# Cross-attention by autocorrelation with a LoRA-mixed feed-forward layer: the two residual adds on GpSimd become accumulating DMAs

## The chip, the cores and the metric

One core of one Trainium2 chip runs the whole kernel. The metric is the device time in microseconds (us). The engines are TensorE (PE in the profile; its weight loads are PEld), VectorE (DVE), ScalarE (ACT), GpSimd (POOL) and SyncE (SP), which here issues every DMA.

## The reference

Cut to what matters, with x and ctx of shape (8, 512, 2048):

```python
def reference(x, ctx, W, bias, A, Bf, coeffs, scales):
    q, v = heads(layernorm(x)), heads(ctx)          # keys and values are both ctx; 8 heads
    corr = irfft(fft(q) * conj(fft(v)))             # over the 512 positions, per column
    w, idx = top_k(corr, int(2 * log(512)))         # 12 lags for each column
    w = softmax(w)
    x = x + sum_i w[i] * v[min(idx[i] + position, 511)]
    h = layernorm(x)
    x = x + h @ W.T + bias                          # the FFN
    x = x + sum_e coeffs[e] * scales[e] * (h @ A[e].T) @ Bf[e].T
    return x
```

## The kernel before

**The work in windows.** A chunk is one batch element and 256 of the 2048 columns, so a batch element has eight chunks and there are 64. The program is one software pipeline of 78 windows and a closing step (`for w in range(windows + 1)` on every engine). Window w transforms chunk w (`values`, `upper`, `queries`), correlates it (`correlate`), picks its lags on VectorE (`choose`), turns the lag weights (`turn_weights`), and finishes chunk w - 1 (`upper_lags`, `lower_lags`, `output`, `part_output`, `store_parts`). From window 14 on, each window also holds an eighth of one batch element's feed-forward product: 96 fp16 matmuls of 128x512 into `f_ps` (`product`; L840, L842 and L844, since W and the normalised rows are each split into a high and a low half). The weights W plus the mixed LoRA update are made in windows 1 to 9.

**The rows.** A batch element has four tiles of 128 rows. Tile i of element b has its turn in window 9 + 8b + i (`row_tile`), so windows 9 to 12, 17 to 20, 25 to 28, 33 to 36 and so on up to 65 to 68 are "row windows", two buffers `rows` taking turns. In such a window SP loads the rows of x, POOL adds the attention (`add_row`), SP stores the sum to DRAM (`store_x1`), DVE takes its mean and variance (`row_statistics`, `row_gain`), ACT normalises it, and its two fp16 halves go to DRAM to come back transposed. The attention's rows come from the DRAM scratch `parts` into the one buffer `attn`, by `load_attn` on SP: the next tile's load is issued right behind the x1 store, ahead of the weights' transposes.

**The groups.** The product's output is finished in groups of 512 columns x 512 rows, one in every second window (`finished_group`). For a group, SP loads the column scales, the bias (broadcast over the partitions) and the stored sum `x1p`; at the end of the window POOL adds the bias to `x1p` (`add_bias`). In the next window DVE scales the product into `y` (`scale_group`), POOL adds it (`add_group`), and SP stores the group and loads the next one into the same buffers.

**Order.** Each engine works through a list written out by hand. Three lists matter here.

POOL in a window: `add_products` (writes `a_prod`), `add_group` if a group is due (in row windows: the second and fourth of a batch element), `add_upper`, `add_lower`, `add_row`, `fold_queries`, `fold_values`, `add_bias` (the first and third row window).

SP, from the row on: `store_x1`, which waits for `row_added`; `load_attn` of the next tile; `turn_weights`, two DMA transposes of `a_w_row` into `a_w_lag` (L515); one pair of weight loads; `load_v`; `store_parts`.

DVE, from `choose` on: `weights_low` (L1338), `row_statistics` (L1372), `part_output` (L1365, L1366; TensorE's `queries` waits for it), `row_gain`, then in the next window `scale_group`, `multiply_queries` (POOL's `add_products` waits for it), `multiply_upper`, `multiply_lower`.

TensorE opens window w + 1 with `upper_lags(w)`, the first matmul of L763, which waits for both transposes of window w.

Of the kernel before, what the change touches and what calls it, by code (L numbers as in the profile page):

```python
# [34 lines left out]
T = 128  # L35
BATCH, L, D = 8, 512, 2048
TB = L // T
WC = 512
# [193 lines left out]
def flow(nc, shared, x, W, A, Bf, coeffs, scales, parts, x1s, hrow, bias, whi, wlo, wscale, out):  # L232
# [12 lines left out]
    with ExitStack() as ctx:  # L245
# [20 lines left out]
        b_in_sb = w_sb[:, 2:4, :].rearrange("p a d -> p (a d)").rearrange("p (e i r) -> p e i r", e=EXPERTS, i=OT)  # L266
        attn = sb("f_attn", [T, D])
        row_hi = sb("f_rowhi", [T, D], F16)
# [5 lines left out]
        y = sb("f_y", [T, TB, WC])  # L274
        x1p = sb("f_x1p", [T, TB, WC])
        scale_sb = sb("f_scale", [T, WC])
        bias_sb = sb("f_bias", [T, WC])
        f_bn = sb("f_bn", [T, 4, 6])
# [131 lines left out]
        x1_out = sem("f_x1_out")  # L410
        attn_in = sem("f_attn_in")
        row_added = sem("f_row_added")
# [12 lines left out]
        y_added = sem("f_y_added")  # L425
        x1p_in = sem("f_x1p_in")
        scale_in = sem("f_scale_in")
        bias_in = sem("f_bias_in")
        bias_added = sem("f_bias_added")
# [41 lines left out]
        def _(sp):  # L471
# [22 lines left out]

            def load_attn(r, early):

                if r >= TILES:
                    return
                at_least(sp, row_added, r)
                if r == 0 and early:  # L500
                    sp.wait_ge(delta_mm, TB * OT)
                cols = slice(0, D) if r % TB else slice(0, D - CH) if early else slice(D - CH, D)
                sp.wait_ge(parts_out, 16 * (CHUNKS * (r // TB + 1) - (r % TB == 0 and early)))
                sp.dma_start(attn[:, cols], part_rows[r * T:(r + 1) * T, cols]).then_inc(attn_in, 16)

            def store_parts(n):
# [11 lines left out]
            def store_x1(w, r):  # L518
                sp.wait_ge(row_added, r + 1)
                sp.dma_start(x1s[r * T:(r + 1) * T, :], rows[w % 2][:, :]).then_inc(x1_out, 16)  # L520
# [37 lines left out]
            def load_group(g):  # L558

                if g >= 4 * BATCH:  # L560
                    return
                b, cols = g // 4, slice(g % 4 * WC, (g % 4 + 1) * WC)
                at_least(sp, y_done, TB * g)
                sp.dma_start(scale_sb[:, :], wscale[cols].partition_broadcast(T)).then_inc(scale_in, 16)
                at_least(sp, bias_added, g)
                sp.dma_start(bias_sb[:, :], bias[cols].partition_broadcast(T)).then_inc(bias_in, 16)
                at_least(sp, out_out, 16 * g)
                sp.wait_ge(x1_out, 16 * TB * (b + 1))
                sp.dma_start(x1p[:, :, :], x1s[b * L:(b + 1) * L, cols].rearrange("(i p) d -> p i d", p=T)
                             ).then_inc(x1p_in, 16)  # L570

            def store_group(g):
                b, cols = g // 4, slice(g % 4 * WC, (g % 4 + 1) * WC)
                if g == 4 * BATCH - 1:
# [70 lines left out]
            for w in range(windows + 1):  # L645
# [5 lines left out]
                load_x(w + 3)  # L651
                if r is not None and r % TB == 0:
                    load_attn(r, False)
                if made:
# [16 lines left out]
                if r is not None:  # L671
                    store_x1(w, r)
                    if r % TB < TB - 1:
                        load_attn(r + 1, True)
                if made:
# [32 lines left out]
                if 1 <= w <= N:  # L708
                    store_parts(w - 1)
                if w >= CHUNKS and w % CHUNKS == 0 and w // CHUNKS <= BATCH:  # L710
                    load_attn(TB * (w // CHUNKS - 1), True)
            sp.wait_ge(out_out, 16 * (4 * BATCH - 1 + TB))
# [397 lines left out]
        def _(pool):  # L1110
# [70 lines left out]
            def add_row(w, r):  # L1181

                pool.wait_ge(rows_in[w % 2], 16 * rows_job(w))
                pool.wait_ge(attn_in, 16 * (r + r // TB + 2))
                add(rows[w % 2][:, :], attn[:, :], ALU.add).then_inc(row_added, 1)

            def add_bias(g):

                pool.wait_ge(x1p_in, 16 * (g + 1))
                pool.wait_ge(bias_in, 16 * (g + 1))  # L1190
                add(x1p[:, :, :], bias_sb[:, :].unsqueeze(1).broadcast_to([T, TB, WC]), ALU.add
                    ).then_inc(bias_added, 1)

            def add_group(g):

                pool.wait_ge(bias_added, g + 1)
                for t in range(TB):
                    pool.wait_ge(y_done, TB * g + t + 1)
                    add(x1p[:, t, :], y[:, t, :], ALU.add).then_inc(y_added, 1)
# [40 lines left out]
        def _(dve):  # L1240
# [127 lines left out]
            def row_statistics(w, r):  # L1368

                dve.wait_ge(row_added, r + 1)  # L1370
                for j in range(4):
# [24 lines left out]
            def scale_group(g):  # L1396

                dve.wait_ge(scale_in, 16 * (g + 1))
                for t in range(TB):
                    dve.wait_ge(product_mm, TB * g + t + 1)  # L1400
                    at_least(dve, y_added, TB * (g - 1) + t + 1)
                    product(y[:, t, :], f_ps[:, t, :], scale_sb[:, :]).then_inc(y_done, 1)

# [142 lines left out]
```

## Time and profile before

| | us |
|---|---|
| median of 3 runs | 2646.56 (2642.76 to 2648.35) |
| span of the profiled execution | 2644.4 |
| TensorE matmuls busy | 2497.7 (94%) |
| GpSimd busy | 2155.5 (82%) |
| VectorE busy | 1901.7 (72%) |
| ScalarE busy | 1055.7 (40%) |
| SP's DMA queue, share of 16 engines' span | 76.6% |

The profiled execution's own span is 2.2 us under the median; no separate device time is given for it. An engine's busy time leaves out waiting, branches and the issuing of DMAs. Matmuls are pipelined and their ends are modelled, so the times between starts say more than durations do. A time to landing of a DMA runs from its issue to its completion.

### The profile page before, as it was taken

Reading aid. Unit: us, or ns where it says so; the run is one execution under the profiler, and the core shown is the slowest. Engines: PE = TensorE matmul, PEld = TensorE weight load, DVE = VectorE, ACT = ScalarE, POOL = GpSimd, SP = SyncE. Lnnn points to the kernel's source line nnn. Section 1 sums busy time; section 2 is a strip of 40 time slices with the busy share of each in tenths; the row PEclk is TensorE's granted clock in tenths of the full one; section 3 lists DMA queues with packets and bytes.
Section 4 is the critical chain, followed back from the end, with each engine's and each line's share of the span. In section 5 each row is a group of like instructions: output and inputs, shape, how many; then the busy total and the mean of one; then the engine's idle time right before and its main releaser. Section 6 shows DMA issues by size and latency. Waiting matters only on the chain.

```text
span 2644.4 us, 36606 instructions
## 1 busy us (share of the span) xinstructions
PE 2497.7 (94%) x12288; PEld 1559.9 (59%) x12288; DVE 1901.7 (72%) x4966; ACT 1055.7 (40%) x1906; POOL 2155.5 (82%) x1558
## 2 busy tenths in 40 slices
PE   4999866799999999999999999999999999999998
PEld 3655555566666656666666666666666666654444
DVE  5989989778787788777877788778876688645000
ACT  4788855533443343533443334533333233201000
POOL 5799999778998799988998899888998899654222
PEclk8999978899999999999999999999999999999999
DMA  9399998966788687966887687957786687758853
GB/s 325 99 261 269 269 244 198 231 192 209 254 266 228 219 252 238 277 203 210 258 270 210 217 275 248 271 181 236 253 250 172 219 265 243 199 203 301 268 180 114
DMA packets 550028, 613.19 MB, mean 232 GB/s; under 512 B 322640, under 2 KB 448720, under 8 KB 532176
## 3 DMA queue, kind: packets, MB, share of 16 engines
q1 hardware_dynamic: 549840, 610.86, 76.6%
q8 instruction: 97, 1.59, 0.2%
q14 instruction: 91, 0.75, 0.1%
HBM read 383.22 MB, written 151.00 MB: 202 GB/s over the span
## 4 chain that ended last, share of the span: by engine, by line
PE 53%; POOL 22%; DVE 8%; DMA 7%; SPq 5%; issue 4%; ACT 1%; POOLq 0%; DVEq 0%; ACTq 0%
PE f_ps L840 11%; PE f_ps L844 11%; PE f_ps L842 11%; PE a_ps L718 7%; PE a_ps L805 5%; PE a_ps L763 4%; POOL a_zu L1115 4%; POOL f_x1p L1115 4%; POOL a_rows L1115 3%; DMA a_w_lag<-a_w_row 2%; PE a_ps L821 2%; PE a_ps L820 2%; POOL a_zv L1115 2%; POOL a_zf L1115 2%; PE a_ps L768 1%
## 5 line engine op out<-in xcount | busy, mean ns | idle before, releaser
L840 PE MATMUL f_ps<-f_whi,f_hhi 128*128 128x512 f16 x2048 | 777.3, 380 | 5.6 <-issue 2.4
L844 PE MATMUL f_ps<-f_whi,f_hlo 128*128 128x512 f16 x2048 | 777.4, 380 | 0.0
L842 PE MATMUL f_ps<-f_wlo,f_hhi 128*128 128x512 f16 x2048 | 777.4, 380 | 0.0
L924 ACT ACTIVATE a_side<-a_ps 128x256 f32<-128x256 f32 (+1 forms) x320 | 128.0, 416 | 873.5 <-PE a_ps L805 698.4
L844 PEld LDWEIGHTS f_ps<-f_whi,f_hlo 128*128 128x128 f16 x2048 | 200.6, 98 | 242.3 <-issue 1.1
L842 PEld LDWEIGHTS f_ps<-f_wlo,f_hhi 128*128 128x128 f16 x2048 | 200.7, 98 | 230.8 <-issue 1.1
L840 PEld LDWEIGHTS f_ps<-f_whi,f_hhi 128*128 128x128 f16 x2048 | 200.7, 98 | 220.6 <-issue 6.7
L1115 POOL TENSOR_TENSOR a_prod<-a_prod,a_tf 128x512 f32<-128x512 f32 x128 | 160.2, 1273 | 138.7 <-DVE a_tf L1242 138.7
L1115 POOL TENSOR_TENSOR a_zv<-a_zv,a_tw 128x512 f32<-128x512 f32 x128 | 183.3, 1450 | 100.5 <-DVE a_tf L1242 100.5
L805 PE MATMUL a_ps<-inv,a_prod 128*128 128x256 f32 x1024 | 239.5, 388 | 25.6 <-POOL a_prod L1115 25.6
L1115 POOL TENSOR_TENSOR f_x1p<-f_x1p,f_y 128x512 f32<-128x512 f32 x128 | 172.7, 1381 | 101.0 <-DVE f_y L1242 101.0
L763 PE MATMUL a_ps<-a_w_lag,lags 128*128 128x256 f16 x1536 | 232.3, 274 | 23.0 <-DMA a_w_lag<-a_w_row 18.0
L805 PEld LDWEIGHTS a_ps<-inv,a_prod 128*128 128x128 f32 x1024 | 198.6, 195 | 65.2 <-POOL a_prod L1115 32.0
L1242 DVE TENSOR_TENSOR f_y<-f_ps,f_scale 128x512 f32<-128x512 f32 x128 | 81.0, 686 | 186.2 <-PE f_ps L844 169.5
L1115 POOL TENSOR_TENSOR f_x1p<-f_x1p,f_bias 128x2048 f32<-128x2048 f32 x32 | 147.5, 4608 | 69.8 <-DMA f_x1p<-x_scratch 69.8
L763 PEld LDWEIGHTS a_ps<-a_w_lag,lags 128*128 128x128 f16 x1536 | 149.7, 98 | 69.0 <-DMA a_w_lag<-a_w_row 23.4
L1115 POOL TENSOR_TENSOR a_zu<-a_zu,a_tu 128x512 f32<-128x512 f32 x128 | 172.3, 1367 | 5.1 <-DVE a_tu L1242 5.1
L1115 POOL TENSOR_TENSOR a_rows<-a_rows,f_attn 128x2048 f32<-128x2048 f32 x32 | 144.2, 4507 | 36.1 <-DMA f_attn<-parts_scratch 36.1
L1115 POOL TENSOR_TENSOR a_zf<-a_zf,a_tf 128x512 f32<-128x512 f32 x128 | 159.2, 1262 | 0.0
L1115 POOL TENSOR_TENSOR a_zu<-a_zu,a_zv 128x512 f32<-128x512 f32 x128 | 158.9, 1257 | 0.0
L718 PE MATMUL a_ps<-a_tv,fold 128*128 128x256 f32 x512 | 129.6, 398 | 26.8 <-ACT a_vk L924 26.8
L1026 ACT ACTIVATE a_rows<-a_rows,f_shift,f_gain 128x2048 f32<-128x2048 f32 x32 | 67.0, 2095 | 218.1 <-DVE f_shift L1384 154.9
(137 smaller groups left out, 5236.6 us busy)
## 6 DMA issues: line engine op xcount, KB each, us to landing
f_whi<-whi_scratch SPq DMA_DIRECT2D x128, 512.0 KB, 5.1
f_wlo<-wlo_scratch SPq DMA_DIRECT2D x128, 512.0 KB, 6.5
a_rows<-in_x_dram SPq DMA_DIRECT2D x62, 1024.0 KB, 8.7
vs<-in_ctx_dram SPq DMA_DIRECT2D x64, 512.0 KB, 6.2
xs<-in_x_dram SPq DMA_DIRECT2D x64, 512.0 KB, 8.0
parts_scratch<-a_so SPq DMA_DIRECT2D x64, 512.0 KB, 7.5
x_scratch<-a_rows SPq DMA_DIRECT2D x32, 1024.0 KB, 5.1
f_x1p<-x_scratch SPq DMA_DIRECT2D x32, 1024.0 KB, 6.8
```

The source lines that it names most:

```text
L718: return nc.tensor.matmul(ps[:, pair, j, :], fold[:, k, :], source, start=True, stop=True)
L763: mm = nc.tensor.matmul(out, lag_mat[:, constant, 2 * cls + k, :], w_lag[:, part, main::TB, :], start=(constant + part == 0), stop=(consta ...
L805: mm = nc.tensor.matmul(corr[:, g, cls * 2 * T:(cls + 1) * 2 * T], prod[:, 2 * k + cls, g * T:(g + 1) * T], inv[:, cls, k, :], start=(k == ...
L820: nc.tensor.matmul(ps[:, 2 + j, i, :], outm[:, k0, :], z[:, s0, :], start=True, stop=False)
L821: mm = nc.tensor.matmul(ps[:, 2 + j, i, :], outm[:, k1, :], z[:, s1, :], start=False, stop=True)
L840: nc.tensor.matmul(f_ps[:, t, :], h_hi[q][:, kq, rows_t], w_hi[u % WR][:, :, kq, :], start=(k == 0), stop=False)
L842: nc.tensor.matmul(f_ps[:, t, :], h_hi[q][:, kq, rows_t], w_lo[u % WR][:, :, kq, :], start=False, stop=False)
L844: mm = nc.tensor.matmul(f_ps[:, t, :], h_lo[q][:, kq, rows_t], w_hi[u % WR][:, :, kq, :], start=False, stop=(k == DB - 1))
L924: return nc.scalar.activation(out, source, ACT.Copy, **how)
L1026: nc.scalar.activation(rows[w % 2][:, :], rows[w % 2][:, :], ACT.Identity, bias=f_shift[:, 0:1], scale=f_gain[:, 0:1]).then_inc(h_done, 1)
L1115: return nc.gpsimd.tensor_tensor(whole, whole, part, op)
L1242: return nc.vector.tensor_tensor(out, a, b, ALU.mult)
```

## The change

`attn` and its loads disappear. `add_row` is now a DMA, issued by GpSimd, that reads 128 rows of `parts` from DRAM and adds them to `rows` in SBUF. `add_bias` is a DMA, issued by GpSimd, that reads the bias broadcast over 128 partitions and four row tiles (the source is 512 rows of 2 KB, 1 MB written) and adds it to `x1p`. `row_added` and `bias_added` are now raised by these transfers' completion. `add_row` also waits for the DMA before it and for the element's parts to be stored in full. `x1p` and the scales have two buffers each, taken in turn by group, so a group's loads wait for the group before the last.

```diff
-        attn = sb("f_attn", [T, D])
-        x1p = sb("f_x1p", [T, TB, WC])
-        scale_sb = sb("f_scale", [T, WC])
-        bias_sb = sb("f_bias", [T, WC])
+        x1ps = [sb(f"f_x1p{i}", [T, TB, WC]) for i in range(2)]
+        scales_sb = [sb(f"f_scale{i}", [T, WC]) for i in range(2)]
...
-            def load_attn(r, early):
...
             def store_x1(w, r):
-                sp.wait_ge(row_added, r + 1)
+                sp.wait_ge(row_added, 16 * (r + 1))
                 sp.dma_start(x1s[r * T:(r + 1) * T, :], rows[w % 2][:, :]).then_inc(x1_out, 16)
...
             def load_group(g):
...
-                at_least(sp, y_done, TB * g)
-                sp.dma_start(scale_sb[:, :], wscale[cols].partition_broadcast(T)).then_inc(scale_in, 16)
-                at_least(sp, bias_added, g)
-                sp.dma_start(bias_sb[:, :], bias[cols].partition_broadcast(T)).then_inc(bias_in, 16)
-                at_least(sp, out_out, 16 * g)
+                x1p = x1ps[g % 2]
+                at_least(sp, y_done, TB * (g - 1))
+                sp.dma_start(scales_sb[g % 2][:, :], wscale[cols].partition_broadcast(T)).then_inc(scale_in[g % 2], 16)
+                at_least(sp, out_out, 16 * (g - 1))
                 sp.wait_ge(x1_out, 16 * TB * (b + 1))
                 sp.dma_start(x1p[:, :, :], x1s[b * L:(b + 1) * L, cols].rearrange("(i p) d -> p i d", p=T)
-                             ).then_inc(x1p_in, 16)
+                             ).then_inc(x1p_in[g % 2], 16)
...
-                if r is not None and r % TB == 0:
-                    load_attn(r, False)
...
                     store_x1(w, r)
-                    if r % TB < TB - 1:
-                        load_attn(r + 1, True)
...
-                if w >= CHUNKS and w % CHUNKS == 0 and w // CHUNKS <= BATCH:
-                    load_attn(TB * (w // CHUNKS - 1), True)
...
             def add_row(w, r):
 
                 pool.wait_ge(rows_in[w % 2], 16 * rows_job(w))
-                pool.wait_ge(attn_in, 16 * (r + r // TB + 2))
-                add(rows[w % 2][:, :], attn[:, :], ALU.add).then_inc(row_added, 1)
+                at_least(pool, row_added, 16 * r)
+                pool.wait_ge(parts_out, 16 * CHUNKS * (r // TB + 1))
+                pool.dma_start(rows[w % 2][:, :], part_rows[r * T:(r + 1) * T, :], accum_op=ALU.add
+                               ).then_inc(row_added, 16)
 
             def add_bias(g):
 
-                pool.wait_ge(x1p_in, 16 * (g + 1))
-                pool.wait_ge(bias_in, 16 * (g + 1))
-                add(x1p[:, :, :], bias_sb[:, :].unsqueeze(1).broadcast_to([T, TB, WC]), ALU.add
-                    ).then_inc(bias_added, 1)
+                cols = slice(g % 4 * WC, (g % 4 + 1) * WC)
+                pool.wait_ge(x1p_in[g % 2], 16 * (g // 2 + 1))
+                pool.dma_start(x1ps[g % 2][:, :, :], bias[cols].partition_broadcast(T).unsqueeze(1).broadcast_to([T, TB, WC]),
+                               accum_op=ALU.add).then_inc(bias_added, 16)
 
             def add_group(g):
 
-                pool.wait_ge(bias_added, g + 1)
+                x1p = x1ps[g % 2]
+                pool.wait_ge(bias_added, 16 * (g + 1))
...
             def row_statistics(w, r):
 
-                dve.wait_ge(row_added, r + 1)
+                dve.wait_ge(row_added, 16 * (r + 1))
```

`scale_group` and `store_group` take the buffer and semaphore of `g % 2` in the same way.

## Rows read from the trace of the kernel before

**Rows 1.** Busy time of each engine in four windows: start:end, length, then each engine.

```profile
687.58:725.57 37.99, 37.99 (x185) 23.86 (x186) 29.29 (x77) 13.04 (x27) 32.49 (x24) 0.96 0.72 235
...
1240.48:1279.62 39.14, 36.46 (x185) 23.05 (x183) 33.89 (x82) 15.91 (x29) 38.83 (x26) 1.00 0.88 284
1279.62:1316.42 36.80, 36.47 (x184) 23.08 (x185) 29.68 (x78) 13.82 (x28) 33.26 (x25) 1.00 0.79 238
...
1389.03:1425.33 36.30, 36.30 (x185) 23.15 (x184) 24.90 (x71) 14.81 (x32) 29.99 (x26) 1.00 0.97 273
```

**Rows 2.** What TensorE waited for from 520 to 2310 us: total, times, longest.

```profile
PE a_ps L763 <- DMA a_w_lag<-a_w_row: 18.0, 10, 4.0
```

**Rows 3.** TensorE's timeline: `upper_lags` opening windows 19, 35, 37; `queries` before one.

```profile
687.58 0.50 PE L763 MATMUL a_ps<-a_w_lag,lags 128*128 128x256 f16 x3 [3.01 <-DMA a_w_lag<-a_w_row]
...
1275.05 1.89 PE L718 MATMUL a_ps<-xs,fold 128*128 128x256 f32 x8
...
1279.62 0.50 PE L763 MATMUL a_ps<-a_w_lag,lags 128*128 128x256 f16 x3 [2.69 <-DMA a_w_lag<-a_w_row]
...
1352.73 0.49 PE L763 MATMUL a_ps<-a_w_lag,lags 128*128 128x256 f16 x3
```

**Rows 4.** SP's timeline, from the x1 store on, in windows 34 and 36.

```profile
1269.76 0.33 SPq L520 DMA_DIRECT2D x_scratch<-a_rows  x1
1270.19 0.38 SPq L504 DMA_DIRECT2D f_attn<-parts_scratch  x1
1270.66 6.88 SPq L515 DMA_TRANSPOSE a_w_lag<-a_w_row  x2
...
1346.23 4.34 SPq L515 DMA_TRANSPOSE a_w_lag<-a_w_row  x2
```

**Rows 5.** POOL's timeline: the four row adds of windows 33 to 36, one bias.

```profile
1224.11 4.51 POOL L1115 TENSOR_TENSOR a_rows<-a_rows,f_attn 128x2048 f32<-128x2048 f32 x1
...
1240.12 4.57 POOL L1115 TENSOR_TENSOR f_x1p<-f_x1p,f_bias 128x2048 f32<-128x2048 f32 x1
1244.66 2.49 POOL L1115 TENSOR_TENSOR a_prod<-a_prod,a_tf 128x512 f32<-128x512 f32 x2
...
1265.23 4.50 POOL L1115 TENSOR_TENSOR a_rows<-a_rows,f_attn 128x2048 f32<-128x2048 f32 x1
...
1300.10 4.51 POOL L1115 TENSOR_TENSOR a_rows<-a_rows,f_attn 128x2048 f32<-128x2048 f32 x1
...
1341.27 4.52 POOL L1115 TENSOR_TENSOR a_rows<-a_rows,f_attn 128x2048 f32<-128x2048 f32 x1
```

**Rows 6.** DVE's timeline: row statistics of windows 33 to 35, and work behind them.

```profile
1231.94 2.46 DVE L1372 BATCH_NORM_STATS2 f_bn<-a_rows 128x6 f32<-128x512 f32 x4
...
1242.76 0.68 DVE L1242 TENSOR_TENSOR a_tf<-a_ps,a_vk 128x512 f32<-128x512 f32 x1
...
1269.77 2.47 DVE L1372 BATCH_NORM_STATS2 f_bn<-a_rows 128x6 f32<-128x512 f32 x4 [1.45 <-POOL a_rows L1115]
...
1273.26 0.68 DVE L1366 TENSOR_TENSOR a_so<-a_ps,a_side 128x512 f32<-128x512 f32 x1
...
1307.39 2.46 DVE L1372 BATCH_NORM_STATS2 f_bn<-a_rows 128x6 f32<-128x512 f32 x4
```

**Rows 7.** DMA issues: count, KB each, median us to landing.

```profile
x_scratch<-a_rows SPq DMA_DIRECT2D x32, 1024.0 KB, 5.1
f_x1p<-x_scratch SPq DMA_DIRECT2D x32, 1024.0 KB, 6.8
...
f_attn<-parts_scratch SPq DMA_DIRECT2D x24, 1024.0 KB, 7.7
```

**Rows 8.** POOL's timeline in window 11, before the product starts.

```profile
421.57 4.50 POOL L1115 TENSOR_TENSOR a_rows<-a_rows,f_attn 128x2048 f32<-128x2048 f32 x1
...
437.87 2.51 POOL L1115 TENSOR_TENSOR a_prod<-a_prod,a_tf 128x512 f32<-128x512 f32 x2 [0.25 <-DVE a_tf L1242]
```

**Rows 9.** TensorE's timeline, in the last batch element's product.

```profile
2470.54 0.38 PE L840 MATMUL f_ps<-f_whi,f_hhi 128*128 128x512 f16 x1 [2.35 <-issue]
```

More of the change, by code:

```diff
@@ L410, in flow @@
         x1_out = sem("f_x1_out")
-        attn_in = sem("f_attn_in")
         row_added = sem("f_row_added")
@@ L425, in flow @@
         y_added = sem("f_y_added")
-        x1p_in = sem("f_x1p_in")
-        scale_in = sem("f_scale_in")
-        bias_in = sem("f_bias_in")
+        x1p_in = [sem(f"f_x1p_in{i}") for i in range(2)]
+        scale_in = [sem(f"f_scale_in{i}") for i in range(2)]
         bias_added = sem("f_bias_added")
@@ L493, in load_rows @@
                 sp.dma_start(rows[w % 2][:, :], x_rows[source * T:(source + 1) * T, :]).then_inc(rows_in[w % 2], 16)
-            def load_attn(r, early):
[L497 to L504, printed above, removed]
             def store_parts(n):
@@ L1183, in add_row @@
                 pool.wait_ge(rows_in[w % 2], 16 * rows_job(w))
-                pool.wait_ge(attn_in, 16 * (r + r // TB + 2))
-                add(rows[w % 2][:, :], attn[:, :], ALU.add).then_inc(row_added, 1)
+                at_least(pool, row_added, 16 * r)
+                pool.wait_ge(parts_out, 16 * CHUNKS * (r // TB + 1))
+                pool.dma_start(rows[w % 2][:, :], part_rows[r * T:(r + 1) * T, :], accum_op=ALU.add
+                               ).then_inc(row_added, 16)
             def add_bias(g):
-                pool.wait_ge(x1p_in, 16 * (g + 1))
-                pool.wait_ge(bias_in, 16 * (g + 1))
-                add(x1p[:, :, :], bias_sb[:, :].unsqueeze(1).broadcast_to([T, TB, WC]), ALU.add
-                    ).then_inc(bias_added, 1)
+                cols = slice(g % 4 * WC, (g % 4 + 1) * WC)
+                pool.wait_ge(x1p_in[g % 2], 16 * (g // 2 + 1))
+                pool.dma_start(x1ps[g % 2][:, :, :], bias[cols].partition_broadcast(T).unsqueeze(1).broadcast_to([T, TB, WC]),
+                               accum_op=ALU.add).then_inc(bias_added, 16)
             def add_group(g):
-                pool.wait_ge(bias_added, g + 1)
+                x1p = x1ps[g % 2]
+                pool.wait_ge(bias_added, 16 * (g + 1))
                 for t in range(TB):
@@ L1396, in scale_group @@
             def scale_group(g):
-                dve.wait_ge(scale_in, 16 * (g + 1))
+                dve.wait_ge(scale_in[g % 2], 16 * (g // 2 + 1))
                 for t in range(TB):
@@ L1401, in scale_group @@
                     at_least(dve, y_added, TB * (g - 1) + t + 1)
-                    product(y[:, t, :], f_ps[:, t, :], scale_sb[:, :]).then_inc(y_done, 1)
+                    product(y[:, t, :], f_ps[:, t, :], scales_sb[g % 2][:, :]).then_inc(y_done, 1)
             def first_statistics(k, source):
```

## The prediction

> **What bounds the kernel now.** I read the busy times of each engine window by window first. With the product running, a window without a row lasts 36.30 us and TensorE is busy for all of it; POOL is busy for 30 [rows 1]. So TensorE sets the pace, and POOL's 82% is no bound by itself. Then the waits of TensorE from 520 to 2310 us, six of the eight batch elements: one kind only, `upper_lags` waiting for the transposed lag weights, 18.0 us in ten waits, 4.0 the longest [rows 2]. All ten follow row windows. That is the place where the row's work touches the clock that counts.
>
> The timelines of window 34 say how. POOL adds the row until 1269.73 [rows 5]. SP stands on `row_added` until then, then issues the x1 store, the load of the next `attn` and only then the transposes, which take SP 6.88 us [rows 4]; the lags start at 1279.62, after 2.69 us of waiting [rows 3]. So 9.9 us lie between the end of the add and the lags. In window 36 no `attn` load stands ahead: the add ends at 1345.79, the transposes take SP 4.34 us [rows 4], and the lags start at 1352.73 without a wait [rows 3, 5]. There 6.9 us are enough.
>
> A stall has a second price. After the wait of 3.01 us at 687.58 the window lasts 37.99 us at a mean granted clock of 0.96 [rows 1, 3]: for part of it TensorE runs at 1.2 instead of 2.4 GHz. That is 1.7 us over 36.30. After 2.69 us the clock stays at 1.00. I charge 1.7 us to each stall of 3 us or more. In the six elements before, that is the one shown and the one of 4.0: 3.4 us. The row windows thus cost 18.0 + 3.4 = 21.4 us over pure TensorE pace. This is nearly all that the change could win there.
>
> **What the change does, part by part.** POOL loses 4.5 us per row and 4.6 us per bias [rows 5]. Inside a row window the row add was the last thing before SP's transposes, so what counts is not POOL's time but the time from the DMA's issue to `row_added`. Call it L; it was 4.5.
>
> No row shows an accumulating DMA, nor one issued by POOL. Below: it can't well beat the fastest plain 1 MB transfer, the x1 store's 5.1 us. Above: two plain passes, since it reads its target as well, 2 x 7.7 = 15.4. The plain read of this very source takes 7.7 at the median [rows 7]. I take L = 10: the plain read, plus about 2.3 for the second operand and for descriptors written by software, between the ends but nearer to 7.7 because a second read of SBUF need not repeat the latency.
>
> The Trainium skill (DMA: Bandwidth & Descriptors, section Bandwidth) gives 6.15 us of DMA time for a plain 1 MB load issued by GpSimd, with a first byte after about 1 us; by that, for a transfer that doesn't accumulate, L would be 7.2, and the sum below would end at about no change. No run here shows it yet.
>
> Now the four row windows of an element, using 33 to 36. POOL reaches the row add at 1224.11, 1265.23, 1300.10 and 1341.27 [rows 5]; the next window opens 6.9 us after `row_added`, or on TensorE's pace, whichever is later.
>
> Window 33: ready at 1224.11 + L + 6.9; TensorE opened at 1240.48 [rows 1]. Stall L - 9.5, for L = 10: 0.5.
>
> Behind it on DVE: the statistics started at 1231.94 [rows 6], so they slip by L - 7.8 = 2.2, and behind them `part_output`, `row_gain`, `scale_group`, `multiply_queries`. The last ended at 1243.44; POOL's `add_products` ran only at 1244.66, behind the bias [rows 5, 6]. With the bias off POOL it gains 1.2 and loses 2.2: POOL is 1.0 later in window 34.
>
> Window 34: ready at 1265.23 + 1.0 + 10 + 6.9 = 1283.1. TensorE's pace is 1279.62 - 2.69 + 0.5 = 1277.4. Stall 5.7.
>
> Window 35 has no group. POOL's add came 20.5 us after the window's opening [rows 3, 5], with DVE's last product of the lags as the releaser, so it stays there: 20.5 + 10 + 6.9 - 36.3 = 1.1.
>
> Window 36: the statistics before it slip by L - 7.3 (1307.39 against 1300.10), less the same 1.2: 1.5. POOL's add stood 25.35 us behind the undelayed opening (1279.62 + 36.30 = 1315.92). Stall 25.35 + 1.5 + 16.9 - 36.3 - 1.1 = 6.35.
>
> Sum per element 13.7, plus 2 x 1.7 for the clock, 17.1; six elements 102.4, less the 21.4 of before: +81. Behind SP's wait for `row_added` stand the transposes, a pair of weight loads, `load_v`, `store_parts` and the next window's `load_x`; the weights loaded there are for the second half of the window after, 18 us away, and hide. Part of the stall may be seen one step earlier: `part_output` ended 4.2 us after the add in window 34 and `queries` starts 1.1 us later (1273.94, 1275.05) [rows 3, 6], so it waits too. It is the same delay, not a second one.
>
> Element 0's rows (windows 9 to 12) meet no product. There from the row add to the next `add_products` it is 16.3 us, all POOL work [rows 8], ended within 0.25 us of DVE. The new path runs over DVE: from the statistics at 1231.94 to the end of the queries' products at 1243.44 it is 11.5, of which the four multiplications of `scale_group`, absent here, are about 2.3 [rows 6]. So L + 9.2 = 19.2, +2.9. Windows 11 and 12 pay it, +6; 9 and 10 also hold a `tile_low` on POOL whose removal from the path about balances it.
>
> Element 7's rows run beside the product alone. No `attn` load is waited for any more, and the group loads no longer hold SP, so the stall of 2.35 at 2470.54 [rows 9] may go: -2.
>
> The bias: POOL can issue it 4.5 earlier than 1240.12, at 1235.6; `add_group` would begin at 1247.1 + 1.0 [rows 5]. Up to 12.5 us of landing are hidden; its like (2 KB runs of 1 MB) takes 6.8 plain [rows 7], 13.6 in two passes. I take 0, with POOL's slack as cover. Second buffers and the dropped waits of SP: 0, since SP's transposes don't wait for them in row windows. The extra traffic rests in L.
>
> Total +81 + 6 - 2 = +85 on a span of 2644.4; on the median, 2646.6 + 85 = 2731 to 2732. I say 2731.
>
> The same sum for other L: 5.1 gives -27; 7 gives -7; 7.3 about 0; 8 gives +23 (stalls 0, 2.2, 0, 3.45; one at the low clock); 12 gives +147 (2.5, 7.7, 3.1, 8.35); 15.4 gives +246.
>
> **Rivals.** *The transfer is as quick as a plain one* (L 5.1 to 7.2). For it: stores of 1 MB take 5.1, and the DMA no longer shares SP's order. Against: the plain read takes 7.7, and this one does more. All row stalls go except 1 to 2 us. Result 2620 to 2642, faster. It decides at L = 7.3.
>
> *A much slower transfer* (L 13 to 15.4): adding in the DMA runs at half the rate, or POOL's writing of descriptors is stretched. For it: the DMA share is already 0.72 to 0.88 in the three row windows shown [rows 1]. Result about 2830 to 2893. The Trainium skill (SBUF — State Buffer, section SBUF: two separate sides) says a VectorE operation in a two-port mode keeps GpSimd from writing the descriptors of its DMAs; that would act here, and no row before can show it.
>
> *The bias is late.* If it lands after 15.4 instead of under 12.5, `add_group` and with it the rows of windows 34 and 36 come 3 us later: 12 x 3 = +36 on top, 2767. For it: 512 runs of 2 KB in the stretch where SP issues weights, values and queries together. Against: 12.5 leaves 5.7 us over the plain landing, more than I charge the row's transfer for its adding.
>
> *Nothing to be measured*: L between 7.2 and 7.5.
>
> **Numbers.** Chances: my forecast (L 8 to 13, bias hidden) 0.53, its own range 2664 to 2830; bias late 0.14; much slower 0.14; quick 0.14; nothing 0.05. Faster by over 0.2% (5 us, about what can be told from no change) 0.14, within 0.05, slower 0.81. The range for 8 in 10 takes in the upper part of the quick case and half of the much slower one: 2635 to 2855.
>
> **What would show it.** L itself: the DMA's issue to landing. `upper_lags` waiting about 6 us after the second and fourth row window of an element and near 1 after the others; windows of 42 to 44 us there, clock 0.96 or less; POOL's busy share down to about 68% (2155.5 less 32 x 9.1); DVE waiting for the DMA before L1372, SP before the x1 store. No stall above 2 us and L near 7 would prove me wrong, as would a wait of TensorE for weights or `h` because the queues are full.

## The result, and the profile after

The changed kernel takes 2740.64 us (median of 4 runs, 2734.85 to 2742.42) against 2644.66 (2641.53 to 2648.35): 1.0357 of the time before, with a 95% interval of 1.0342 to 1.0372. That is 96 us slower; the prediction said 2731. The profiled executions stand 94.3 us apart. One run of `e7_best` took 5345.51 us, twice its three others, and is left out of its time below.

```profile
span 2738.7 us, 36462 instructions
...
PE 2534.0 (93%) x12288; PEld 1577.1 (58%) x12288; DVE 1894.6 (69%) x4966; ACT 1055.7 (39%) x1906; POOL 1924.3 (70%) x1558
```

GpSimd lost 231 us of busy work and the kernel became slower. First the windows 33 to 37, which answer to [rows 1]: start:end, length, each engine's busy time with instructions, granted clock, DMA share, GB/s.

```profile
1233.71:1270.01 36.30, 36.30 (x185) 23.15 (x184) 31.08 (x92) 10.45 (x22) 27.63 (x24) 1.00 0.62 175
1270.01:1314.52 44.51, 38.20 (x185) 24.04 (x184) 31.23 (x80) 13.64 (x28) 32.44 (x26) 0.96 0.90 263
1314.52:1350.82 36.30, 36.30 (x185) 23.18 (x184) 30.52 (x79) 15.33 (x28) 28.72 (x23) 1.00 0.82 232
1350.82:1395.62 44.80, 39.66 (x186) 24.92 (x185) 31.37 (x81) 13.95 (x28) 32.11 (x26) 0.93 0.92 271
1395.62:1432.16 36.54, 36.54 (x185) 23.33 (x184) 27.10 (x63) 24.16 (x41) 28.19 (x22) 0.99 0.92 266
```

The first and third row windows stand at TensorE's pace. The second and fourth, which also hold a group add, last 44.5 and 44.8 us. In all six batch elements it is these twelve windows, 42.5 to 45.7 us each; together they last 533.0 us, against 455.2 before. They account for 77.8 of the 94.3 us; the tail behind the last window with attention work gives 8.6, the rest of the windows about 8.

What TensorE waited for from 520 to 2391 us (total, times, longest), beside [rows 2]:

```profile
PE a_ps L697 <- DVE a_so L1348: 42.8, 12, 4.9
PE a_ps L799 <- POOL a_zu L1094: 26.2, 20, 2.6
PE a_ps L742 <- DMA a_w_lag<-a_w_row: 0.4, 1, 0.4
```

The transposes, on which TensorE had waited 18.0 us, are almost gone from the list. The delay now shows one step earlier, twelve times, as `queries` waiting for `part_output` (a_so), and there is a wait of another kind: `output` for POOL's `a_zu`. TensorE's timeline in window 34 has both:

```profile
1297.53 0.67 PE L799 MATMUL a_ps<-a_zu,outm 128*128 128x256 f32 x2 [1.41 <-POOL a_zu L1094]
...
1311.29 3.39 PE L697 MATMUL a_ps<-xs,fold 128*128 128x256 f32 x8 [4.89 <-DVE a_so L1348]
1314.52 0.49 PE L742 MATMUL a_ps<-a_w_lag,lags 128*128 128x256 f16 x3
```

The window is 8.21 us too long: 6.30 of waiting, and 1.90 because its matmuls are busy for 38.20 instead of 36.30 us. Most of these 1.90 are in one row: the eight matmuls of `queries` take 3.39 us after the wait, where they took 1.89 before [rows 3]. The granted clock over them is 0.55: TensorE fell from 2.4 to 1.2 GHz behind a wait of 4.89 us. (Windows with a wait show 36.5 to 36.7 us of busy matmuls at a clock of 1.00 too, so 0.2 to 0.4 of the 1.90 is not the clock.)

Why `part_output` is late, on POOL, beside [rows 5]:

```profile
1265.78 1.28 POOL L1172 DMA_DIRECT2D f_x1p<-in_L_ffn_bias_dram  x1
1273.06 2.50 POOL L1094 TENSOR_TENSOR a_prod<-a_prod,a_tf 128x512 f32<-128x512 f32 x2 [6.01 <-DVE a_tf L1224]
1279.22 7.00 POOL L1094 TENSOR_TENSOR f_x1p<-f_x1p,f_y 128x512 f32<-128x512 f32 x4 [3.66 <-DMA f_x1p<-in_L_ffn_bias_dram]
...
1297.33 0.60 POOL L1165 DMA_DIRECT2D a_rows<-parts_scratch  x1
```

The bias was issued at 1265.78 and landed at about 1279.2, 13.4 us later. The group add waited 3.66 us for it, everything behind it moved back, and the row's DMA went out at 1297.33, 27.3 us into the window. The 7.00 us of the group add are no loss beside the kernel before; the section on the early bias shows why. SP, beside [rows 4], in windows 33 and 34:

```profile
1261.21 0.32 SPq L505 DMA_DIRECT2D x_scratch<-a_rows  x1
1261.62 4.40 SPq L500 DMA_TRANSPOSE a_w_lag<-a_w_row  x2
...
1306.96 0.33 SPq L505 DMA_DIRECT2D x_scratch<-a_rows  x1
1307.39 4.35 SPq L500 DMA_TRANSPOSE a_w_lag<-a_w_row  x2
```

The x1 store follows `row_added` at once, so issue to `row_added` is 27.50 - 19.94 = 7.56 us in window 33 (issue at 1253.65) and 36.95 - 27.32 = 9.63 in window 34. And DVE, beside [rows 6]:

```profile
1261.47 2.46 DVE L1354 BATCH_NORM_STATS2 f_bn<-a_rows 128x6 f32<-128x512 f32 x4
...
1280.29 2.35 DVE L1376 TENSOR_TENSOR f_rowlo<-a_rows,f_rowhi 128x2048 f16<-128x2048 f32 x1
```

In window 33 the statistics start without a wait: a row transfer of 7.56 us is wholly hidden there. The DMA issues, beside [rows 7] (count, KB each, median us to landing), and the queues (packets, MB, share of 16 engines):

```profile
q1 hardware_dynamic: 539472, 568.91, 68.9%
q0 software_dynamic: 21504, 67.11, 13.4%
...
a_rows<-parts_scratch POOLq DMA_DIRECT2D x32, 1024.0 KB, 8.3
x_scratch<-a_rows SPq DMA_DIRECT2D x32, 1024.0 KB, 4.3
f_x1p<-x_scratch SPq DMA_DIRECT2D x32, 1024.0 KB, 9.1
f_x1p<-in_L_ffn_bias_dram POOLq DMA_DIRECT2D x32, 1024.0 KB, 14.0
```

### The profile page after: what moved, and what is told of

Same layout as the page of the kernel before. It is cut to its first block and busy times, and to the rows that moved or that the text cites. A ratio compares the mean times of both kernels' runs of the same rounds, so it can differ in the third digit from the quotient of the medians.

```text
span 2738.7 us, 36462 instructions
## 1 busy us (share of the span) xinstructions
PE 2534.0 (93%) x12288; PEld 1577.1 (58%) x12288; DVE 1894.6 (69%) x4966; ACT 1055.7 (39%) x1906; POOL 1924.3 (70%) x1558
## 3 DMA queue, kind: packets, MB, share of 16 engines
q0 software_dynamic: 21504, 67.11, 13.4%
## 5 line engine op out<-in xcount | busy, mean ns | idle before, releaser
L1094 POOL TENSOR_TENSOR f_x1p<-f_x1p,f_y 128x512 f32<-128x512 f32 x128 | 182.3, 1454 | 268.6 <-DMA f_x1p<-in_L_ffn_bias_dram 165.1
L697 PE MATMUL a_ps<-xs,fold 128*128 128x256 f32 x512 | 146.4, 437 | 65.2 <-DVE a_so L1348 65.1
L1354 DVE BATCH_NORM_STATS2 f_bn<-a_rows 128x6 f32<-128x512 f32 x128 | 79.1, 681 | 153.4 <-DMA a_rows<-parts_scratch 152.9
L697 PEld LDWEIGHTS a_ps<-xs,fold 128*128 128x128 f32 x512 | 109.3, 219 | 98.3 <-issue 66.4
L1094 POOL TENSOR_TENSOR a_zu<-a_zu,a_tu 128x512 f32<-128x512 f32 x128 | 159.8, 1270 | 4.6 <-DVE a_tu L1224 4.6
```

The costliest lines, as they stand in the source:

```text
L697: return nc.tensor.matmul(ps[:, pair, j, :], fold[:, k, :], source, start=True, stop=True)
L1094: return nc.gpsimd.tensor_tensor(whole, whole, part, op)
L1354: op = nc.vector.bn_stats(f_bn[:, j, :], rows[w % 2][:, j * WC:(j + 1) * WC])
```

## The experiments

The theory after this reading (A): two costs, the row's transfer between row and transposes, and the bias that lands too late for the group add; the bias is the larger. The rivals: (B) the row's transfer alone makes the loss, because it adds and is slow, and the bias only follows; (C) the order behind the row on SP and DVE makes it, and neither transfer would cost anything elsewhere. These letters are of this section; each recorded expectation has its own. The ratios are to the kernel before, run beside each experiment (medians of 2645.64 to 2648.12 us).

### One part alone

`e1_row_only`: the row by DMA, the bias by POOL as before (with two x1p buffers).

```diff
-                pool.dma_start(x1ps[g % 2][:, :, :], bias[cols]...broadcast_to([T, TB, WC]),
-                               accum_op=ALU.add).then_inc(bias_added, 16)
+                pool.wait_ge(bias_in, 16 * (g + 1))
+                add(x1ps[g % 2][:, :, :], bias_sb[:, :].unsqueeze(1).broadcast_to([T, TB, WC]), ALU.add
+                    ).then_inc(bias_added, 1)
```

> The row is added by the DMA as in the changed kernel, the bias is loaded by SP and added by GpSimd as before (x1p keeps its two buffers, the scales have one). Theory A, the row's latency and a late bias both cost: in the row windows with a group, GpSimd issues the row about 2.5 us earlier in the window than in the changed kernel (it no longer waits for the bias), twelve times, and the small waits of output() in the other group windows go: 2740 - 30 - 8 = about 2700 to 2706. Theory B, only the row's latency costs (as the prediction has it, bias at nothing): about 2740. Theory C, the bias is the main part: under 2670.

`e2_bias_only`: the kernel before, with only `add_bias` made a DMA (one x1p buffer).

```diff
-                pool.wait_ge(bias_in, 16 * (g + 1))
-                add(x1p[:, :, :], bias_sb[:, :].unsqueeze(1).broadcast_to([T, TB, WC]), ALU.add
-                    ).then_inc(bias_added, 1)
+                pool.dma_start(x1p[:, :, :], bias[cols]...broadcast_to([T, TB, WC]),
+                               accum_op=ALU.add).then_inc(bias_added, 16)
```

> The kernel before, with the bias alone added by a DMA that GpSimd issues (one x1p buffer, rows added by GpSimd from attn). Theory A: the bias lands some 13 us after its issue, add_group begins 2 to 4 us later in every group window, and in the row windows with a group the lag weights' transposes and so TensorE come later by that: +35 to +60 us, 2680 to 2705. Theory B: GpSimd loses 4.6 us per group and the bias is hidden: 2635 to 2645. Theory C: over 2710.

Measured: the row alone 2659.2 us, 1.0043 (1.0026 to 1.0059), so about +11; the bias alone 2740.14 us, 1.0355 (1.0334 to 1.0375), so +94 by the ratio, as much as the whole change. Both lie where the expectations put the bias as the main part (under 2670, over 2710), and outside the 2700 to 2706 and 2680 to 2705 that I favoured. Window 34 of the row alone, then its waits of TensorE from 540 us:

```profile
1245.99:1284.37 38.38, 36.70 (x185) 23.00 (x184) 30.30 (x78) 12.86 (x27) 32.73 (x27) 1.00 0.89 273
```

```profile
PE a_ps L701 <- DVE a_so L1352: 18.9, 12, 2.5
PE a_ps L746 <- DMA a_w_lag<-a_w_row: 8.5, 13, 2.1
```

No wait is above 2.5 us, and the granted clock is 0.99 or 1.00 in the twelve second and fourth row windows. It is 0.97 in window 21 and 0.96 in window 27, which together last 2.8 us more than 36.30 each. Window 27 opens after a wait of 2.13 us, with one of 1.46 shortly ahead of it; before, a single wait of 2.69 us left the clock at 1.00. So the length of one wait doesn't tell what the clock does. Window 34 of the bias alone, on POOL:

```profile
1266.45 1.32 POOL L1188 DMA_DIRECT2D f_x1p<-in_L_ffn_bias_dram  x1
...
1280.54 4.94 POOL L1112 TENSOR_TENSOR f_x1p<-f_x1p,f_y 128x512 f32<-128x512 f32 x4 [8.17 <-DMA f_x1p<-in_L_ffn_bias_dram]
...
1296.60 4.49 POOL L1112 TENSOR_TENSOR a_rows<-a_rows,f_attn 128x2048 f32<-128x2048 f32 x1
```

The row add is POOL's own, and starts at 29.8 us into the window instead of 24.75 [rows 5], because the group add waits 8.17 us for the bias. TensorE's waits from 520 to 2391 us:

```profile
PE a_ps L817 <- POOL a_zu L1112: 63.6, 15, 6.2
PE a_ps L760 <- DMA a_w_lag<-a_w_row: 13.1, 6, 3.7
```

So the late group add holds TensorE in two ways: through `add_upper` and `add_lower` behind it on POOL, which write the `a_zu` that `output` needs, and through the row. Here the first is the larger. B falls. The parts don't add up (11 + 94 against 96): with one x1p buffer the bias can go out only 0.38 us ahead of window 34; with two, 4.23 ahead. The second buffer thus gives the bias's DMA a start of some 4 us. That this closes the sum is argued, since no run has the bias alone with two buffers.

### The bias issued earlier

`e4_bias_early`: the changed kernel, with the bias's DMA ahead of `add_upper` in the same window, some 28 us earlier.

```diff
+                if at and at[1] % 2 == 1:
+                    add_bias(4 * at[0] + at[1] // 2)
                 if 1 <= w <= N:
                     add_upper(w - 1)
...
-                if at and at[1] % 2 == 1:
-                    add_bias(4 * at[0] + at[1] // 2)
```

> The changed kernel with the bias DMA issued on GpSimd ahead of add_upper in the same window instead of at the window's end, so that it has some 30 us to land. Theory A: the wait of add_group for the bias (165 us in all) goes, rows are issued some 2.5 us earlier in twelve windows: 2700 to 2710. Theory B: no change, 2740, or worse where GpSimd now waits for x1p in front of add_upper.

Measured: 2673.92 us, 1.01 (1.0082 to 1.0118). One moved issue gives back 67 of the 96 us, twice what was expected (2700 to 2710). The transfer is hardly quicker (12.1 us at the median against 14.0), but nobody waits for it; window 34 has the row-only kernel's 38.40 us, and the row's DMA goes out 23.65 us into the window and lands 8.08 later, against 27.32 and 9.63. TensorE's waits from 540 us:

```profile
PE a_ps L697 <- DVE a_so L1348: 19.2, 12, 3.1
PE a_ps L742 <- DMA a_w_lag<-a_w_row: 8.4, 13, 2.2
PE a_ps L742 <- DVE a_tf L1224: 0.3, 1, 0.3
```

The waits for `a_zu` are gone as well. The group add now takes 4.96 us instead of 7.00, but the add behind it takes longer by as much, as it does with the row alone:

```profile
1258.74 4.54 POOL L1094 TENSOR_TENSOR a_zu<-a_zu,a_tu 128x512 f32<-128x512 f32 x2
```

In the changed kernel this add took 2.49 us. DVE's `f_rowlo` (1280.29 above) falls on one of the two adds in either case and costs it 2.05 us. So the whole 3.67 us by which the row's DMA goes out later (27.32 against 23.65) is the group add's wait for the bias. The late bias costs that, 1.5 us in this row's transfer, and the low clock. The kernel is still 15 us above the row alone, 9 of them behind the last window with the attention's work: that tail lasts 347.6 us in the changed kernel, 348.6 here, 339.2 with the row alone and 339.0 before.

### What makes the two transfers long

`e3_row_plain`: the row's DMA without `accum_op`, otherwise the changed kernel. x's own part of the residual is left out.

```diff
-                pool.dma_start(rows[w % 2][:, :], part_rows[r * T:(r + 1) * T, :], accum_op=ALU.add
-                               ).then_inc(row_added, 16)
+                pool.dma_start(rows[w % 2][:, :], part_rows[r * T:(r + 1) * T, :]).then_inc(row_added, 16)
```

> The changed kernel, but the row's DMA overwrites the row of x instead of adding to it (the residual of x is left out). It tells what the adding costs within the transfer. Theory A: little, the plain load of the same bytes took 7.7 us to landing before and this one takes 8.3 to 9.6: L shorter by about 0.5 us, twelve windows, 2730 to 2736. Rival: the second operand makes up the 2.3 us that the prediction charged for it and more: L near 6, 2700 to 2715.

Measured: 2694.56 us, 1.0177 (1.0161 to 1.0193). Issue to `row_added` is 5.10 us in window 33 and 7.46 in window 34, against 7.56 and 9.63: adding costs the transfer 2.2 to 2.5 us, and about 46 us of the kernel when the bias is late as well. Both expected ranges (2730 to 2736, 2700 to 2715) were too high; the rival was nearer.

`e8_bias_plain`: the bias's DMA without `accum_op`; x and the attention are left out of those outputs. `e9_bias_rows`: its source is 512 different runs of x1 in DRAM instead of one 2 KB run read 512 times; the bias is left out and x1 counts twice.

```diff
-                pool.dma_start(x1ps[g % 2][:, :, :], bias[cols].partition_broadcast(T).unsqueeze(1).broadcast_to([T, TB, WC]),
-                               accum_op=ALU.add).then_inc(bias_added, 16)
+                # e8_bias_plain: the same call without accum_op
+                # e9_bias_rows: source x1s[g // 4 * L:(g // 4 + 1) * L, cols].rearrange("(i p) d -> p i d", p=T)
```

> The changed kernel, but the bias DMA overwrites x1p instead of adding to it (x and the attention are left out of the result). It tells what the adding costs in this transfer, which lands 13.4 us after its issue. If the adding is the main cost (as 2.5 us of 7.6 is in the row's transfer), it lands within 9 to 10 us and the run comes near the one with the early bias, 2675 to 2690. If the 512 runs of 2 KB and the traffic are, it still lands after 12 us or more: 2715 to 2740.

> The changed kernel, but the bias DMA adds 512 different runs of 2 KB (the stored x1, once more) instead of the same 2 KB read 512 times; the bias is left out of the result and x1 counts twice. It tells what makes this transfer land after 13 to 14 us. If reading one 2 KB place over and over is slow, it lands within 8 to 10 us and the run is at 2675 to 2700. If the short runs or the traffic around are the cause, it lands after 12 us or more as before: 2715 to 2745.

Measured: 2722.95 us, 1.0285 (1.027 to 1.0301), and 2731.96 us, 1.0334 (1.0313 to 1.0355), both in the second of the two ranges that were expected. The medians to landing of the bias's DMA, first plain, then from different rows:

```profile
f_x1p<-in_L_ffn_bias_dram POOLq DMA_DIRECT2D x32, 1024.0 KB, 12.5
```

```profile
f_x1p<-x_scratch POOLq DMA_DIRECT2D x32, 1024.0 KB, 13.8
```

Neither the adding (1.5 us) nor the repeated source (0.2) makes it late. What is left is what the three have in common: 1 MB in 512 runs of 2 KB on GpSimd's queue, in the stretch where SP issues weights, values and queries. The queue counts 144 packets for each row and 528 for each bias (4608 with the row alone, 16896 with the bias alone). The number of packets by itself doesn't set the time: in `e8_bias_plain` a bias has 272 (13312 packets less the rows' 4608, over 32) and lands only 1.5 us sooner. The stretch isn't the main cause either, since 28 us earlier in the window (`e4_bias_early`) it still takes 12.1. SP's load of `x1p`, also 1 MB in runs of 2 KB and plain, takes 9.1 in the changed kernel. What share the run length, the queue and the traffic have was not separated further.

### The order behind the row

`e5_late_both`: the changed kernel, with SP's transposes ahead of the x1 store, so that they don't stand behind `row_added`, and `part_output` ahead of the row statistics on DVE. `e6_before_late`: the same two moves in the kernel before (`load_attn` moves with the store). `e7_best`: both moves and the early bias.

```diff
-                if r is not None:
-                    store_x1(w, r)
                 if turned_by_dma(w):
                     turn_weights(w)
+                if r is not None:
+                    store_x1(w, r)
...
-                if r is not None:
-                    row_statistics(w, r)
                 if 1 <= w <= N:
                     part_output(w - 1)
+                if r is not None:
+                    row_statistics(w, r)
```

> The changed kernel with two moves that take row_added off TensorE's path: SP stores x1 behind the weights' transposes instead of ahead of them, and VectorE writes the output halves (part_output) ahead of the row's statistics. Theory A (a late row reaches TensorE only through these two waits; the late bias delays the row issue): the waits of queries() on a_so and the late lags go, what is left is the output() matmuls' wait for GpSimd, late through the bias: even row windows at 38 to 40 us instead of 44.5, about 2665 to 2685. Rival (the late bias holds TensorE by itself, through the product sums of GpSimd): above 2710.

> The kernel before with the same two moves (the next attn load moves with the x1 store). Theory A: the 18.0 us of waits for the transposes and the clock's 3.4 us go, so 2622 to 2630. Rival: the row windows are held by GpSimd's own load in any case, and it stays at 2640 to 2648.

> The changed kernel with both moves and the bias DMA issued ahead of add_upper. Theory A: no wait of TensorE between windows 14 and 62 is left, every window 36.3 us (1780 for these 49 instead of 1806 before): 2620 to 2635, if the last windows lose nothing; it then tells whether the accumulating DMAs gain anything over the kernel before with the same moves. Rival: DMA traffic in the row windows delays weights or transposes: 2645 or more.

Measured: 2767.38 us (2742.33 to 2778.76), 1.0419 (1.0366 to 1.0473); 2644.02 us, 0.9984 (0.9973 to 0.9995); 2662.43 us, 1.0053 (1.0036 to 1.007). Theory A of the expectations failed all three times; the rivals' ranges held, for `e5_late_both` and `e6_before_late` by other mechanisms than they name. In the kernel before all of the twelve second and fourth row windows become 37.57 us, and with the early bias eleven. In the changed kernel itself the same moves make it worse, with the widest spread of all: window 36 lasts 56.05 us, and TensorE waits for the transposes nine times, up to 14.8 us. Its SP and POOL timelines, then two stretches of it:

```profile
1388.96 18.45 SPq L500 DMA_TRANSPOSE a_w_lag<-a_w_row  x2
1415.69 0.33 SPq L505 DMA_DIRECT2D x_scratch<-a_rows  x1
```

```profile
1390.26 0.59 POOL L1165 DMA_DIRECT2D a_rows<-parts_scratch  x1
```

```profile
1390.00:1400.00 10.00, 9.55 (x37) 6.21 (x38) 1.29 (x2) 0.60 (x1) 9.67 (x10) 0.83 1.20 192
1400.00:1416.00 16.00, 2.74 (x13) 1.80 (x11) 0.30 (x1) 0.00 (x0) 2.42 (x2) 0.75 1.24 79
```

The row's transfer went out 1.3 us behind the transposes' issue and took 25.4 us; SP's two transposes took 18.45 us instead of 4.4. In the second stretch the DMA engines count as busy for 1.24 of their time and move 79 GB/s. Taking the order's cost away doesn't help as long as the bias is late, since the row's transfer then meets the transposes. So `e5_late_both` doesn't settle C, as the moves bring a cost of their own. What speaks against C is `e7_best` beside `e6_before_late`: with the same order and an early bias the two transfers still cost 18 us, 9 of them in the tail (348.3 against 339.5). What is right in C is that a late row reaches TensorE by way of this order: with both moves no wait for `a_so` is left in any of the three kernels. Where the bias was early or on POOL (`e7_best`, and `e11_early_sp` and `e12_row_only_sp` below), the row's DMA of windows 34 and 36 went out 2.2 to 3.5 us ahead of them and took 7.5 to 8.5 us.

`e10_before_sp`: the kernel before, with SP's move alone. `e11_early_sp`: the changed kernel with the early bias and SP's move. `e12_row_only_sp`: the row by DMA, the bias on POOL, and SP's move. Their edits are the first half of the diff above, on those kernels.

> The kernel before with one move: SP stores x1 and loads the next attn behind the weights' transposes; VectorE's order stays. The two moves together left a wait of 1.27 us in every even row window and about 30 us in all, on VectorE, because part_output then waits for ScalarE where the statistics had filled the time. Theory A: the wait for the transposes goes and nothing takes its place: windows 14 to 62 in about 1780 us instead of 1806, 2620 to 2627. Rival: part_output, 4.2 us behind the row's add, holds queries() next: 2632 to 2645.

> The changed kernel with the bias DMA issued early and the x1 store behind the transposes; VectorE's order stays. Theory A: in the even row windows row_added comes at about 32 us into the window, part_output 4.2 later, so queries() still waits some 2 us: windows of 38 to 39, twelve of them, 2655 to 2672. Rival: the row's transfer is now in flight with the transposes, which in the run with both moves took 25 us when they met: some windows of 45 us or more, above 2700.

> Only the row by DMA, the bias added by GpSimd, and the x1 store behind the transposes. Against the kernel before with the same move it tells what the row's DMA is worth by itself. Theory A: queries() waits about 2 us for part_output in twelve windows, where the kernel before with the move waits for nothing: 2640 to 2655, 15 to 30 us slower than it. Rival: GpSimd's freed 4.5 us per row pay: within 5 us of it or faster.

Measured: 2661.85 us, 1.0066 (1.0049 to 1.0082); 2654.76 us, 1.0041 (1.0027 to 1.0055); 2648.54 us, 1.0015 (1.0004 to 1.0025). The second is at the lower edge of its range; the first is above both of its ranges, and so the third, expected 15 to 30 us slower than it, is 13 us faster. The row by DMA thus costs 0.15% (0.04 to 0.25) over the kernel before once SP's transposes don't wait for it. That it beats POOL's add in the same order is because the move hurts the kernel before in an unexpected place: all row windows run at 36.30, and the window behind an element's fourth row lasts 44.4 to 45.9 in five of six elements. Window 37 of it on DVE, then POOL:

```profile
1354.69 13.00 DVE L1394 TENSOR_TENSOR f_rowlo<-a_rows,f_rowhi 128x2048 f16<-128x2048 f32 x1
```

```profile
1354.37 0.72 POOL L1115 TENSOR_TENSOR a_zu<-a_zu,last 1x256 f32<-1x256 f32 x1
1355.06 2.48 POOL L1115 TENSOR_TENSOR a_zv<-a_zv,a_tw 128x512 f32<-128x512 f32 x2
...
1365.62 3.20 POOL L1149 TENSOR_TENSOR xs<-a_tq 128x512 f32<-128x512 f32 x1
```

DVE's instruction takes 13.00 us where the median of its 28 is 2.75 and the shortest 2.28. POOL was 0.3 us ahead of it and then had work without a gap. In POOL's row at 1365.62 one of its kind takes 3.20 us where the one behind it takes 1.26, and 1354.69 + 13.00 is in the middle of it, so that DVE seems to have got in there for its 2.3 us. By this reading it was held for 10.7 us, by seven groups of POOL's in a row, and `choose` and all behind it came that much later.

## Why the prediction was right or wrong

**The path and the total were right, the split was not.** TensorE sets the pace, the loss sits in the second and fourth row windows at 42.5 to 45.7 us with the clock at 0.92 to 0.97, and POOL's busy share fell to 70%. The total was +85 predicted, +94 in the traces. Two terms of the sum were mis-sized, in opposite directions, and that they nearly cancel is luck. The forecast's own case (L of 8 to 13, the bias hidden) didn't occur: L was at or under its lower edge and the bias was not hidden; where it is (`e4_bias_early`), the kernel is at +26.

**The term that failed: "The bias: ... I take 0".** The landing was taken as 12.5 us or less because its like from SP takes 6.8 [rows 7]. It is 13.4 us in window 34 and 14.0 at the median, and 12.5 even without adding. The cover was taken as 12.5 too and is 9.8: POOL issues the bias 4.2 us ahead of the window (predicted 4.9), and is free for the group add 5.6 us into it (5.5 in `e4_bias_early`), because `add_products` comes earlier, not later. That is most of the loss: 67 us come back when it goes out earlier, 81 when POOL adds it. The rival "the bias is late" had the place and the landing nearly right, but priced only the wait (3 us a window), on top of a row that costs 10. It missed what a later group add sets off: `output` waits for `a_zu` (26.2 us, and 63.6 with the bias alone), the row's transfer goes out 3.7 us later in window 34 and takes 1.5 more (8.9 against 8.2 as a mean of the twelve windows), and the clock falls in all of them, where with the row alone it fell to 0.96 or 0.97 in two of the windows from 15 to 62.

**L, taken as 10.** Measured 7.6 in window 33, and 7.3 to 8.0 in the other first and third row windows; in the second and fourth a mean of 8.2 with the row alone and 8.9 with the bias beside it (8.1 and 9.6 in window 34). Beside the rows of elements 0 and 7 it was 7.5 to 13.1. The sum's own line for L = 8 has stalls of 0, 2.2, 0 and 3.45, a mean of 2.8 in the two that stall; with the row alone these twelve windows exceed 36.30 by 31.7 us, 2.64 each. That line gave +23 with 1.7 for a low clock in one window of each element, 10 us in all; the clock fell in two windows for 2.8 us, and the kernel came out at +11. Without the late bias, "quick" and "nothing" were thus nearer than the forecast: no result here is faster, but the row's part is +0.43%. The Trainium skill's rate (DMA: Bandwidth & Descriptors, section Bandwidth), by which a transfer that doesn't accumulate would take an estimated 7.2, is above the plain 5.10 and 6.6 at the median, and near the 7.56 of the adding one.

**DVE's slip of 2.2 us** in window 33 didn't happen, since 7.56 is under the 7.8 that the statistics had to spare. The gain by the bias leaving POOL did: `add_products` comes 3.05 us into window 34 instead of 4.18.

**The clock.** I charged 3.4 us before and 20.4 after. Windows 15 to 62 exceed 48 x 36.30 by 107.5 us, of which TensorE's waits are 69.4, so longer matmuls 38; before, 23.8 with 18.0 [rows 2] and 6. Most of the 38 is the clock; 0.2 to 0.4 us in each window with a wait is not. So waits grew by 51 (predicted 82.2 - 18.0 = 64) and the rest by 32 (predicted 17, all clock): in window 36 the matmuls are 3.36 us longer, twice what I took from one row.

**Where the stall shows.** I expected `upper_lags` to wait 6 us and said part of it might be seen at `queries`. What comes by the row is nearly all there (42.8 us against 0.4); the 26.2 us of waits for `a_zu` I didn't expect. `upper_lags` and `queries` both hang on `row_added`, by SP and by DVE, and `queries` comes first.

**The ends.** Element 0 was charged +6; windows 9 to 13 together are 1.5 us longer, and the stretch from 1 to 14 only 0.7, since the windows behind take it back. Element 7's tail was -2 and is +8.6. There the group add waits 22.30 us for the bias, the row's DMA stands behind it on POOL, and SP's weight loads stand behind `row_added`. TensorE and SP at the end of it:

```profile
2552.02 0.61 PE L819 MATMUL f_ps<-f_whi,f_hhi 128*128 128x512 f16 x1 [6.40 <-DMA f_wlo<-wlo_scratch]
```

```profile
2536.91 0.33 SPq L505 DMA_DIRECT2D x_scratch<-a_rows  x1
...
2537.91 0.54 SPq L530 DMA_DIRECT2D f_wlo<-wlo_scratch  x1
```

The prediction had named "a wait of TensorE for weights" as a thing that would prove it wrong; here it is one wait of 6.4 us. The weights of the third row took 14.1 us to land, at 2552.0, where the median of their kind is 7.0; at that pace they would have been there as TensorE came. So busy queues have their part in it beside SP's order, as the prediction feared; no run separates the two. The tail is 334.9 to 339.5 in every kernel with POOL's bias, and 346.4 to 348.6 with the bias's DMA, early or late, but 341.7 where that DMA doesn't add and 340.4 where the row's doesn't. So most of it needs the adding transfer of the bias, moving its issue doesn't cure it, and why a plain row does is open.

**The fixed part.** No version is clearly better than the kernel before; its own order with both moves is 0.16% faster, within what the prediction called no change. What both moves still pay, 1.27 us in each second and fourth row window, is TensorE's wait for DVE's products of the lags (13.1 us in twelve waits, 1.1 at most).

## What to carry to other kernels

Before an engine's add is given to an accumulating DMA, find who waits for it and how long ago it can be issued: an add of 4.5 us became 7.3 to 9.7 us for rows of 8 KB in the middle six elements (up to 13.1 in the first and last) and 12 to 14 us for runs of 2 KB, and the engine time saved bought nothing, since TensorE's own work filled the windows. Issue it as soon as its operands allow; here the place of one line in a list was worth 67 us. And take the price of a transfer from a row of the same run length and the same issuing queue, or keep twice its value in the range, with what is queued behind its waiter.

## What the runs showed of the hardware that was not expected

- **On GpSimd's queue the adding cost less than whatever sets the bias apart from the row.** 1 MB in 8 KB runs: 5.1 us plain, 7.6 adding, in window 33. 1 MB in 2 KB runs: 12.5 plain, 14.0 adding, medians. POOL itself is taken for 0.60 us by the row's issue and 1.3 by the bias's.
- **A row transfer in flight with DMA transposes** (`e5_late_both`, the twelve second and fourth row windows). Where the row's DMA went out 0.5 to 1.1 us ahead of the transposes (three windows) it took 9.1 to 9.5 us. Where it went out 0.1 to 1.3 us behind them (nine) it took 15.5 to 25.4 in six and 8.3 to 10.7 in three. SP's transposes took up to 19.7 us instead of 4.4. Why three of the nine escape wasn't found.
- **DVE and POOL exclude each other on some instructions, and POOL's run isn't interrupted.** DVE's f_rowlo (two SBUF inputs) takes 2.28 us alone; a POOL add that starts 0.16 us behind it takes 4.48 instead of 2.49 us, thus waits for its end. A group add (four instructions) in which it falls takes 7.00 instead of 4.95. The other way round, DVE's instruction took 13.00 us beside seven of POOL's groups in a row, and some 13 us in four other elements of `e10_before_sp`. The Trainium skill (SBUF — State Buffer, section SBUF: two separate sides) has this as an exclusive lock of a shared port pair, held by whoever comes first for its instruction; the 4.48 agrees, and the 13.00 suggests that a loser can miss the pair for many instructions of the other. That this lock delays the writing of a DMA's descriptors, as the prediction weighed, no run here shows: in windows 34 to 36 the row's DMA is issued 10 to 18 us after f_rowlo. In element 7 two of its issues overlap f_rowlo (2475.31 and 2525.65), and these transfers take 11.8 and 11.2 us, against 11.7 for one that doesn't (2496.27).
- **Two small moves can undo each other.** SP's transposes ahead of the x1 store cure all row windows of the kernel before and cost 8 to 9.5 us in the window behind; with DVE's move as well, neither happens.
